# An adaLN attention and FP4 feed-forward block on one core: both rows' statistics in one BN_STATS, v's high part on ScalarE, deeper input buffers, and new instruction orders

## The reference

```
h = layernorm(x) * (1 + ca) + sa
q, k, v = h @ Wq + bq, ...            # reshaped to (b, 16 heads, 8, 256)
attn = softmax(einsum('bhdt,bhds->bhts', k, v) * temperature)   # over s
x = x + ga * einsum('bhdt,bhts->bhds', q, attn)
h = layernorm(x) * (1 + cb) + sb
gate, up = fp4_linear(h, w_gate), fp4_linear(h, w_up)           # width 352
x = x + gb * fp4_linear(silu(gate) * up, w_down)
```

## Time and profile before

| | |
|---|---|
| median of 3 runs | 685.01 us (680.25 to 691.11) |
| profiled execution | 680.49 us |
| its span, first to last instruction | 678.7 us |
| mean granted TensorE clock | 0.925 of full speed |
| busy: DVE / ACT / PE / POOL | 593.7 / 566.9 / 559.9 / 515.3 us |

### The profile page before, as it was taken

One profiled execution on the slowest core, in us unless ns is written; L12 is line 12 of the kernel. 1 busy time (PEld: TensorE's weight loads), 2 busy tenths in 40 slices (PEclk: granted clock), 3 DMA queues, 4 the chain that ended last, 5 costly groups with the idle time before them and its releaser, 6 DMA issues.

```text
span 678.7 us, 15600 instructions
## 1 busy us (share of the span) xinstructions
PE 559.9 (83%) x4336; PEld 382.8 (56%) x4336; DVE 593.7 (87%) x1331; ACT 566.9 (84%) x2281; POOL 515.3 (76%) x655
## 2 busy tenths in 40 slices
PE   4578787999888898879888989888898889878763
PEld 2355355666665565656666656655666666655343
DVE  5578489999999998999999999999899999989451
ACT  2288598999999997989998999999899999989211
POOL 2014746888887887878888688988788888876884
PEclk9568798999999997999998999999899999999766
DMA  3545435455555644665554555554555555550100
GB/s 112 150 119 133 126 86 145 127 141 139 141 151 156 150 129 115 146 156 132 146 146 132 156 148 145 146 144 118 153 141 150 145 145 144 136 138 25 33 8 24
DMA packets 87873, 86.14 MB, mean 127 GB/s; under 512 B 8550, under 2 KB 83532, under 8 KB 87788
## 3 DMA queue, kind: packets, MB, share of 16 engines
q1 hardware_dynamic: 87344, 84.94, 47.9%
q10 hardware_dynamic: 444, 0.20, 0.1%
HBM read 47.29 MB, written 37.81 MB: 125 GB/s over the span
## 4 chain that ended last, share of the span: by engine, by line
POOL 27%; DVE 24%; issue 18%; PE 12%; DMA 9%; SPq 5%; ACT 3%; DVEq 1%; ACTq 0%; POOLq 0%
DVE neg_max L632 7%; POOL hid_q L394 5%; DMA k_stack<-split_dram 4%; POOL hid_q L398 4%; DMA split_dram<-kv_lo 4%; POOL rstd L316 3%; PE score_ps L887 3%; PE bank L929 3%; POOL h_c L323 3%; DVE hid L747 3%; SPq L225 3%; DVE hid_am L598 3%; POOL h_c L329 3%; POOL h L336 2%; ACT probs L485 2%
## 5 line engine op out<-in xcount | busy, mean ns | idle before, releaser
L485 ACT ACTIVATE probs<-score_ps,neg_max 128x256 f32<-128x256 f32 x1024 | 472.8, 492 | 23.5 <-DVE neg_max L632 21.2
L632 DVE TENSOR_REDUCE neg_max<-score_ps 128x4 f32<-128x1024 f32 x256 | 309.1, 1208 | 17.8 <-PE score_ps L887 17.2
L887 PE MATMUL score_ps<-v_stack,k_stack 128*128 128x256 f32 x1024 | 217.6, 332 | 58.3 <-DMA k_stack<-split_dram 39.4
L485 ACT ACTIVATION_READ_ACCUMULATOR probs<-score_ps,neg_max 128x1 f32 x1024 | 229.0, 224 | 0.0
L887 PEld LDWEIGHTS score_ps<-v_stack,k_stack 128*128 128x128 f32 x1024 | 153.9, 200 | 129.1 <-ACT probs L485 62.4
L929 PE MATMUL bank<-probs,q_z 128*32 128x256 f32 x2048 | 140.6, 394 | 11.9 <-POOL q_z L349 11.8
L929 PEld LDWEIGHTS bank<-probs,q_z 128*32 128x32 f32 x2048 | 54.5, 111 | 66.4 <-POOL q_z L349 29.4
L949 PE MATMUL bank<-wgu_T,h_T 128*128 128x352 f32 x128 | 55.9, 523 | 16.5 <-issue 16.5
L978 PE MATMUL bank<-wd_T,hid_T 118*128 118x128 f32 x384 | 60.1, 298 | 5.0 <-ACT hid_T L519 4.6
L978 PEld LDWEIGHTS bank<-wd_T,hid_T 118*128 118x128 f32 x384 | 52.6, 207 | 10.0 <-ACT hid_T L519 9.2
L398 POOL TENSOR_TENSOR hid_q<-hid_q,hid_mag 128x704 f32<-128x704 f32 x32 | 53.9, 1685 | 2.5
(11 more groups left out here) (104 smaller groups left out, 916.7 us busy)
## 6 DMA issues: line engine op xcount, KB each, us to landing
split_dram<-kv_hi SPq DMA_DIRECT2D x128, 128.0 KB, 2.4
split_dram<-kv_lo SPq DMA_DIRECT2D x128, 128.0 KB, 2.4
v_stack<-split_dram SPq DMA_DIRECT2D x32, 512.0 KB, 4.3
k_stack<-split_dram SPq DMA_DIRECT2D x128, 128.0 KB, 4.6
mod_bc<-mod_dram SPq DMA_DIRECT2D x32, 256.0 KB, 3.9
x_in<-in_L_attn_x_dram SPq DMA_DIRECT2D x32, 128.0 KB, 3.5
out_dram<-out_t SPq DMA_DIRECT2D x32, 128.0 KB, 2.1
w_mod<-in_L_wmod_dram SPq DMA_DIRECT2D x1, 384.0 KB, 3.3
```

What stands on the lines that cost most here:

```text
L485: nc.scalar.activation(probs[p][:, h, a, :], score_ps[:, h % 4, a, :], ACT.Exp, bias=neg_max[:, p, n:n + 1], accum_out=row_sum[:, p, h, a: ...
L632: nc.vector.tensor_reduce(neg_max[:, p, 4 * u:4 * u + 4], score_ps[:, lo:lo + 2, :, :].rearrange("p b a n -> p (b a) n"), AX.X, ALU.max, n ...
L887: last = nc.tensor.matmul(score_ps[:, h % 4, a, :], k_stack[p][:, h, 128 * a:128 * a + 128], v_stack[p][:, h // R, :], start=True, stop=True)
```

## The change

- `stats1_rows` and `stats2_rows`: one BN_STATS reads both rows interleaved (`by_row`). BN_STATS keeps even and odd elements apart, so its six outputs are count, mean and sum of squared deviations of row 0 and the same of row 1. The BN_AGGRs go; `variance1` and `variance2` make that sum / 128 + eps in one instruction; the two instructions for minus the mean go, since POOL now subtracts the mean that lies in the statistics.
- `v_hi` moves from DVE to ACT. `k_hi` waits for it, since both read one PSUM bank.
- `x_in` and `mod_bc` get six places, each with a semaphore of its own.
- The weights are quantised and transposed in three parts (gate, up, down) of 384, 384 and 352 columns, spread over steps 1 to 9.
- For the first two elements, the stores of v and half of the loads of `k_stack` are issued by ACT's queue.
- Banks are given out anew, and every engine's list in `step` is a new one. `STAGES` is 11 where it was 10.

```diff
-STAGES = 10
+NX = 6
+STAGES = 11
...
+        def by_row(x):
+
+            return x.rearrange("p a f -> p f a")
...
             def stats1_rows(b, c):
-                wait_dma(dve, x_loaded, b)
-                for a in range(2):
-                    nc.vector.bn_stats(stats1[:, a, :], x_in[:, c, a, :]).then_inc(stat_a, 1)
...
+                wait_in(dve, x_loaded, b)
+                wait_batches(dve, xn_made, b - 1, 2)
+                nc.vector.bn_stats(stats1[:, c % 2, :], by_row(x_in[:, b % NX, :, :])).then_inc(stats1_made, 1)
+
+            def variance1(b, c):
+                dve.wait_ge(stats1_made, b + 1)
                 wait_batches(dve, rstd1_made, b)
-                wait_batches(dve, xn_made, b, 2)
-                nc.vector.tensor_scalar(ve1[:, :], mv1[:, :, 1], EPS, None, ALU.add).then_inc(ve1_made, 1)
-                nc.vector.tensor_scalar(nm1[:, :], mv1[:, :, 0], -1.0, None, ALU.mult).then_inc(nm1_made, 1)
+                nc.vector.tensor_scalar(var1[:, :], stats1[:, c % 2, 2:6:3], 1.0 / D, EPS, ALU.mult, ALU.add)\
+                    .then_inc(var1_made, 1)
...
+            def v_hi(b, c):
+                wait_batches(act, kv_ps_made, b + 1)
+                wait_dma(act, split_stored, b - 2, STORES * 16)
+                nc.scalar.activation(halves(kv_hi[c % 2][:, 1, :]), kv_rows(1), ACT.Copy).then_inc(v_hi_made, 1)
...
             def k_hi(b, c):
-                wait_batches(dve, kv_ps_made, b + 1)
+                wait_batches(dve, v_hi_made, b + 1)
...
+                at(k, 5, gate1)
+                at(k, 7, hid_scale)
+                at(k, 7, hid_recip)
+                at(k, 1, stats1_rows)
+                at(k, 1, variance1)
...
+                at(k, 5, stats2_rows)
+                at(k, 5, variance2)
+                at(k, 4, maxes, 6)
+                at(k, 4, maxes, 7)
+                at(k, 7, hid_exponent)
+                at(k, 2, k_hi)
+                at(k, 2, v_lo)
```

More of the change, by code:

```diff
@@ L21 @@
 NW = 2 * 3 * D + FF
+FFC = (slice(0, 3 * D), slice(3 * D, 6 * D), slice(6 * D, NW))
+FFB = tuple(slice(s.start // QB, s.stop // QB) for s in FFC)
 EPS = 1e-5
@@ L420, in step @@
-            def step(k):
-                at(k, 4, h2_y)
-                at(k, 0, rstd1_pow)
-                at(k, 4, h2_add)
-                at(k, 6, hid_rescale)
-                at(k, 7, residual2)
-                at(k, 4, h2_sub)
-                at(k, 0, normalise1)
-                at(k, 4, h2_rescale)
-                at(k, 3, residual1)
-                at(k, 5, hid_y)
-                at(k, 3, rstd2_pow)
-                at(k, 3, normalise2)
-                at(k, 3, scale2)
-                at(k, 3, shift2)
-                at(k, 5, hid_add)
-                at(k, 5, hid_sub)
-                at(k, 2, q_scaled)
+                nc.gpsimd.tensor_tensor(blocks16(hid_q[:, :]), blocks16(hid_q[:, :]),
+                                        spread16(hid_sc[:, :]), ALU.mult).then_inc(hid_dq_made, 1)
@@ new lines, in ff_rescale @@
+            def ff_rescale(i):
+                pool.wait_ge(ff_fp4[i], 8)
+                w = blocks16(w_ff[:, FFC[i]])
+                nc.gpsimd.tensor_tensor(w, w, spread16(w_sc[:, FFB[i]]), ALU.mult).then_inc(ff_fp4[i], 1)
+            def step(k):
+                if k == 4:
+                    ff_sub(0)
+                if k == 3:
+                    ff_y(0)
+                at(k, 9, residual2)
+                if k == 3:
+                    ff_add(1)
+                if k == 4:
+                    ff_sub(1)
+                at(k, 5, residual1)
+                at(k, 7, hid_y)
+                if k == 4:
+                    ff_rescale(1)
+                if k == 4:
+                    ff_rescale(0)
+                if k == 3:
+                    ff_y(2)
+                if k == 6:
+                    ff_rescale(2)
+                at(k, 5, rstd2_pow)
+                at(k, 5, normalise2)
@@ L438, in step @@
                 if k == 1:
                     zero_q()
-                if k == 2:
-                    ff_weights_scaled()
+                at(k, 5, scale2)
+                at(k, 5, shift2)
+                at(k, 7, hid_add)
+                at(k, 7, hid_sub)
+                at(k, 4, q_scaled)
+                at(k, 5, h2_y)
+                at(k, 5, h2_add)
+                if k == 4:
+                    ff_add(2)
+                at(k, 7, hid_rescale)
+                if k == 5:
+                    ff_sub(2)
@@ new lines, in step @@
+                at(k, 7, hid_magic)
+                if k == 2:
+                    ff_scale(1)
+                at(k, 2, k_lo)
+                at(k, 3, maxes, 0)
+                if k == 1:
+                    zero_k(0)
+                if k == 4:
+                    ff_magic(2)
+                at(k, 5, h2_max)
+                at(k, 8, gate2)
+                at(k, 5, h2_scale)
+                at(k, 3, maxes, 1)
+                at(k, 4, row_sums_inv)
+                if k == 3:
+                    ff_exponent(0)
```

663 lines of the change are left out of this document (356 added, 307 removed).

## The result

The changed kernel took 725.69 us (median of 4 runs, 724.22 to 726.66) against 686.73 us of the kernel before (4 runs, 680.25 to 691.11): 1.060 times as long, with an interval of 1.052 to 1.068. Forecast were 720 us, in a range of 655 to 742. The profiled span is 722.4 us.

The account below looks back on a forecast made before the run. DVE was taken to bound; 17.25 us plus waits for POOL made 20.13 per interval. 46.9 + 31 x 20.13 - 8.4 + 8 + 48.2 = 718.7 us of span, plus 1.8: 720 us, range 655 to 742.

Parts of the forecast that it names:

- the row of 1.30 us: DVE's scale of h, 0.165 us at best, took 1.30 in the old profile, ending just after POOL's hid_sub.
- the 0.26 us of the prediction: On DVE, how much too late h2_scale was forecast to reach the gap ahead of POOL's hid_sub.
- The other collisions: DVE waiting for POOL per element: variance2 0.96 us, hid_exponent 0.38, hid_magic 0.11; hid_scale nothing.
- Rival 4: On DVE, BN_STATS over interleaved rows runs at half rate: +0.4 us per element, 730 us; chance 0.14 together with rival 3.
- DVE's own 17.25 us: DVE's forecast interval per element after the change without port collisions, down from 17.94 us.
- PE's slack: PE and ACT have over 2 us of slack, so moved work, banks and later k_stack loads cost nothing.
- rival 3: PE pauses behind mix, waiting for q, and its clock falls: 735 to 750 us; chance 0.14 together with rival 4.
- The 8 us that I kept for disturbance: Allowance in the whole time, kept of the old kernel's 24.5 us, mostly start-up and waits for x_in.
- Start and end: Time outside the 31 intervals: start-up 46.9 us, 3 less than before, and unchanged drain of 48.2 us.
- Rival 1: DVE and POOL do not collide, ACT bounds at 17.6 to 17.95 us: 650 us, up to 661; chance 0.22.
- Rival 2: Only one of the two large DVE-POOL collisions comes about: 676 to 691 us, no change; chance 0.12.
- the full 8.4 us: Collisions absent in the first four intervals, where hid isn't there yet: 4 x 2.1 us taken off.

Follow-up runs that it names:

- e8_nm_only: The changed kernel with the mean negated by DVE again and added by POOL instead of subtracted; 723.5 us, ratio 1.059 to the kernel before.
- e9_reorder_sub: The changed kernel with DVE's list in the order of e7_reorder, POOL still subtracting, no negated mean on DVE; 732.74 us, ratio 1.075 to the kernel before.
- e1_hsc: The changed kernel with h2_scale one place later on DVE, behind maxes 1; 689.99 us, ratio 1.010 to the kernel before.
- e7_reorder: The changed kernel with DVE negating the mean, POOL adding it, and DVE's list laid out anew against POOL's; 669.66 us, ratio 0.984 to the kernel before.
- b6_all_old_order: The kernel before, old order, with single BN_STATS without BN_AGGR, v's high part on ACT, six places and earlier x_in; 677.64 us, ratio 0.991.
- e2_var2: The changed kernel with variance2 behind maxes 6 instead of ahead; 729.21 us, ratio 1.066 to the kernel before.
- b2_sub: The kernel before with subtract in place of add in POOL's normalise1 and normalise2; 706.13 us, ratio 1.032 to the kernel before.
- e6_nm: The changed kernel with DVE negating the mean, POOL adding it, and h2_scale behind maxes 1; 687.18 us, ratio 1.010 to the kernel before.

## Why the prediction was right

1. **The exclusion (the row of 1.30 us).** Right, and it is the cause. The collision of `h2_scale` with `hid_sub` was priced at 1.43 us and measures 1.45; taking 1.21 of it away gave some 35 us, against 44 by the step (31 x 1.43). The margin was thinner than the 0.26 us of the prediction: `h_sc` starts 0.07 to 0.10 us behind `hid_sub` in every steady interval (470.54 against 470.46 above), so that this collision came about at all is in part luck. The Trainium skill, "SBUF — State Buffer", section "Who interferes with whom", has a `tensor_scalar` in the two-port mode and a GpSimd instruction waiting for each other's whole instructions; the timelines agree, with DVE's records ending 0.02 to 0.04 us after POOL's. They agree for `hid_y` against `variance2` too (464.16 behind 464.13), the pair that no row of before showed, so that an instruction on two elements is caught as well.
2. **The other collisions.** `variance2` was priced at 0.96 and waits 0.71; the exponent of hid at 0.38, for the end of `scale2`, and waits 0.15, ending (467.01) before `scale2` does (467.58); magic of hid at 0.11 and waits nothing. `hid_scale` was priced at nothing and waits 0.46, for `residual2`. I had POOL idle there; it was late by then, behind slower normalisations, and with these fast again (e8_nm_only) `hid_sc` is back at 0.17. The sum was right (2.77 against 2.88), but of its five parts only the first was, and that the others cancel is luck.
3. **The statistics.** The slot of a BN_STATS of 256 elements was taken as 0.34 us, half-rate reading as 0.54. In e9_reorder_sub, where the instruction behind is independent, it measures 0.34 (573.18 to 573.52); in the change, with a dependent one behind, 0.41 and 0.48 (462.31 to 462.72, 462.80 to 463.28), so the 0.12 for a dependent pair was about right too. Rival 4 is out. DVE's own 17.25 us holds: 17.25 + 2.77 = 20.02, and 0.20 idle ahead of `gate2` make 20.22, where the undisturbed interval has 20.17.
4. **POOL's work.** Wrong. The prediction took 15.7 us per element from before and did not price the subtraction as another operation. It costs 4 x 0.35 = 1.4 us there. In the changed order giving it back gains 2 us at most (e8_nm_only), since a wait moves to `variance1` and the clock falls more often; in the relaid order it is worth 63 us.
5. **PE's slack.** "PE and ACT have over 2 us of slack ... cost nothing" failed in one place. The wait of `mix` for q was seen and priced as rival 3, at 0.5 to 1 us for each element. The wait came in every interval, the fall of the clock in every fourth, at 1.24 us (21.4 - 20.17), seven times in the steady part, 9 us in all. The 8 us that I kept for disturbance stood in the sum for another reason and happened to cover this, which is luck; waits for `x_in` and the stacks, which I had in mind, are gone.
6. **Start and end.** 48.9 and 50.8 us against 46.9 and 48.2: 4.6 us too little together; the intervals came 0.9 us under the forecast, and the span 3.7 us above it. The longer end goes with the new lists (50.7 us in e1_hsc and 50.3 in e7_reorder, 48.6 in b6_all_old_order); its cause is open.

Rival 1 (no collision, 650 us) needed h_sc near 0.17 us, and e7_reorder shows what it is worth: with the collisions nearly gone the interval is 18.29, not 17.6, by the reading above since the ring over POOL, PE and DVE then sets it. Rival 2 is e1_hsc: 690 us against its 676 to 691. The lower end of that range takes off the full 8.4 us although one of the collisions is gone; by its own terms 4 x (2.1 - 1.43) = 2.7 us come off, and it is 682.

## What to carry to other kernels

Where two engines exclude each other, lay the new order of the one beside the other's and look for the gaps; a start 0.1 us too late for one cost 1.45 us per element here. A wait that is taken away by moving one instruction often reappears at the next (e2_var2, e8_nm_only), so the places of all exclusive instructions have to be laid out together, as in e7_reorder. And an instruction saved by folding it into another engine's is not free until that engine's new operation has been timed.

## What the runs showed of the hardware that was not expected

- On POOL the operation sets the time of a TENSOR_SCALAR: subtract and multiply 0.80 us, add and multiply 0.45, for 128x128 f32 with two per-partition operands (b2_sub against the kernel before, and e8_nm_only against the change).
- TensorE's clock went from 2.4 to 1.2 GHz in steady intervals in which no single pause is longer than 2.4 us. With a pause for q of 1.1 us (e1_hsc) or 1.43 us (e7_reorder) in each interval it did so in none of 25 steady intervals, with 1.77 us (e8_nm_only) in 11, with 2.12 us (e9_reorder_sub) in all, and with 2.23 us in 7 (the change) and 16 (e2_var2). In e6_nm no pause in the steady part is longer than 1.01 us (0.86 for q), and yet it did so in 6, for instance behind this pause of 0.89 us, where six matmuls of `down_proj` take 1.31 us and not 0.83. So the length of the single pause does not tell it, and what decides is open.

```profile
252.94 0.67 PE L1041 MATMUL bank<-hT,w_q 128*128 128x256 f32 x2 [0.89 <-DVE kv_lo L773]
...
253.57 1.31 PE L1107 MATMUL bank<-wd_T,hid_T 118*128 118x128 f32 x6
```

- POOL's own instructions are lengthened in turn: in the interval shown, `shift2` (L387) took 1.08 us, while DVE's magic of hid ran (467.64 to 468.15). In e9_reorder_sub, where no DVE instruction of the kind stands beside it, it took 0.73.
